# Two sums of value products moved by one step of ten on VectorE, in a decoder layer's output-projection group

## The chip, the cores and the metric

One core of one Trainium2 chip. The metric is the device time of one execution in microseconds (us); the time before the change is the median of three runs.

## The reference

A decoder layer over x of 8 batches x 512 tokens x 256 channels, in float32, three steps with a residual each:

```python
x = x + attn(layernorm(x), Wq, Wk, Wv, Wo)        # 16 heads, causal, complex-valued: q, k, v have 32 numbers a head
x = x + xattn(layernorm(x), ctx, ctx)             # per token: 16 query heads x 16 key heads, causal over heads
x = x + ffn(layernorm(x), kernel, bias, a, b)     # y = h @ int4(kernel) + bias + (h @ a) @ b
```

In `xattn` each token attends over its own 16 heads of 16 numbers: scores = q.k over the 16 numbers, masked so that head q sees keys k <= q, a softmax over k, and the sum of probability times value over k. No two tokens meet there.

## The kernel before, in words

One pass of `body(i, b)` runs per batch index i from -1 to 7, on every engine with the same structure (passes 3 to 5 are one hardware loop). A pass has four groups g of four attention heads each, and each group ten steps n, in which TensorE makes ten pairs of "units": one exponential unit (scores on the key side, for group g) and one maximum unit (scores on the query side, for the group after). Each batch is at several stages at once: in pass i, group 1 does the output projection of batch i-1's attention, the per-token attention (`xattn`) of the tiles of batches i-1 and i-2, and the projections of batch i+1.

The maxima. At step n >= 1 TensorE scores maximum unit n-1 into one of two PSUM banks (`scores`, L619), and VectorE takes its maximum in the same step (`take_max`, L1240, instruction L1251). TensorE scores unit u only after the maximum of unit u-2 has been taken (`max_taken`). Unit 9 is done in step 0 of the next group, and two small minima (L1312, L1313) finish the row. TensorE then turns the row (L659).

The split. At steps 1 and 2 TensorE projects q and k of the next heads into PSUM banks misc[0] and misc[1]; ScalarE copies the high part, and VectorE makes the low part at steps 2 and 3 (`low_part`, L1257: q_lo, k_lo). SyncE moves six pieces by DMA into stack_q and stack_k, where the maximum and exponential units read them. A bank of misc is taken by the next user only when its last reader is done (`take`, L528): in group 2 the value projection of step 3 (`project_v`, L605, writing misc<-w_hi,xt_hi) takes the bank that q_lo reads.

The per-token attention is shared between GpSimd and VectorE. GpSimd makes score products (L325), VectorE sums them (L1263, score_rows) at steps 5 and 8 and adds the mask to the diagonal blocks at step 9 (L1360, reads score_rows and head_mask), then takes the row maxima (L1382). GpSimd subtracts them (L1646), ScalarE does the exponential, VectorE sums and inverts (`tile_inverses`, L1279 and L1282, at step 2), GpSimd normalises (L1628) and makes the value products in four instructions, chunks 0 to 3 (L1633). VectorE sums these over the keys in the next group (`value_sums`, L1271, instruction L1263, head_out), chunk 3 first, and GpSimd adds head_out to x2 (`add_to_x2`, L1599, instruction L1601), which waits for the semaphore hpv_sum that VectorE raises after chunks 0 and 1. On GpSimd's queue that add stands ahead of the normalisation and the value products of the next tile.

The order of the work is written out by hand: each engine runs its own list in program order. In groups 0, 2 and 3 the value sums stand in step 0. In group 1 (`late_sums`, L1324) step 0 and step 1 also carry the adds of the output projection to x1 (L1288) and steps 1 and 2 the layernorm statistics of x1 (L1229, L1235, L1237), so there the value sums start at step 1. GpSimd turns the statistics into coefficients (`ln_coefficients`, L1562, ends with L1570) ahead of its add to x2. Passes 2 to 7 have value sums in group 1, six groups; pass 7 has no q and k projections, and so no q_lo and k_lo, in that group.

Of the kernel before, what the change touches and what calls it, by code (L numbers as in the profile page):

```python
# [97 lines left out]
def decoder_layer(nc, x, ctx_in, wq, wk, wv, wo, ffn_w, ffn_bias, ffn_a, ffn_b, out):  # L98
# [26 lines left out]
    def ok(b):  # L125
        return 0 <= b < N_BATCH

    with ExitStack() as ctx:
# [184 lines left out]
        def tiles(i, g):  # L313
            def tile(back):
                b, t = divmod(g - back, NT)
                return (b - 1, t) if ok(i + b - 1) else None
            return tile(2), tile(3), tile(4)
# [836 lines left out]
        def _(dve):  # L1154
# [68 lines left out]
            def ln_statistics(which, src, part):  # L1223

                if part == 0:

                    wait(dve, ln_scale[which], n_scale[which].up() - 1)
                for t in (2 * part, 2 * part + 1):
                    last = vec.bn_stats(ln_raw[:, which, t, :], src[:, t, :])  # L1229
                if part == 0:  # L1230
                    return
                last.then_inc(dve_own, 1)

                dve.wait_ge(dve_own, n_own.up())
                vec.tensor_copy(touched[:, which, :], ln_raw[:, which, 0, 0:1])  # L1235
                for t in range(NT):
                    last = vec.bn_aggr(ln_mv[:, which, t, :], ln_raw[:, which, t, :])  # L1237
                last.then_inc(ln_stats[which], 1)
# [32 lines left out]
            def value_sums(chunks):  # L1271
                return sum_products(
                    lambda j: head_out[:, j * 4 * HD:(j + 1) * 4 * HD],
                    lambda j: pv_prod[:, COFF[j]:COFF[j + 1]].rearrange("p (a k) -> p a k", k=4 * (j + 1)), chunks)
# [16 lines left out]
            def body(i, b):  # L1291
                for g in range(NG):
                    st = stages(i, g)
                    scored, attended, added = tiles(i, g)
                    for n in range(UNITS):
# [28 lines left out]
                        late_sums = g == 1 and ok(i - 1)  # L1324
# [11 lines left out]
                        if g == 1 and ok(i - 1) and n in (1, 2):  # L1336
                            dve.wait_ge(x1_added, n_wo.now(2 - n))
                            ln_statistics(1, x1, n - 1)
                        if added and n == (1 if late_sums else 0):
                            value_sums((2,))  # L1340
                        if added and n == (2 if late_sums else 0):
                            value_sums((0, 1)).then_inc(hpv_sum, 1)
                        if attended and n == 2:
                            tile_inverses()
# [154 lines left out]
            for c in range(CC):  # L1499
                last = vec.tensor_tensor(first_rows(by_row(w_lo, c)), first_rows(by_head(w_raw, c)),  # L1500
                                         f32(first_rows(by_row(w_hi, c))), ALU.subtract)
            last.then_inc(w_lo_ready, 1)
            turn.batches(dve, body, N_BATCH)


# [243 lines left out]
```

## Time and profile before

| | us |
|---|---|
| median of 3 runs | 806.22 |
| the runs | 806.05, 806.22, 807.44 |
| profiled execution | 807.63 |
| its span | 805.8 |
| TensorE busy | 746.7 |
| VectorE busy | 603.2 |
| GpSimd busy | 493.2 |
| ScalarE busy | 403.6 |

The profile is of one execution; its span runs from the first to the last instruction, and times on it are in us from the span's start. PE is TensorE, PEld its weight loads, DVE VectorE, ACT ScalarE, POOL GpSimd, SP SyncE. A row of a timeline gives the start, the time that the merged instructions cover, the engine, line, operation, output<-inputs, the count, and in brackets the idle time ahead of it with the one that ended it.

### The profile page before, as it was taken

To read this page: it belongs to the slowest core of one execution; us is meant where nothing else is said; L and a number is where in the kernel's file an instruction comes from. 1 tells how busy PE (TensorE), PEld (TensorE's weight loads), DVE (VectorE), ACT (ScalarE), POOL (GpSimd) and SP (SyncE) were. 2 spreads that over 40 slices of the span, in tenths; PEclk is the share of its full clock that TensorE was granted. 3 is DMA by queue.
4 is the path that set the end of the run, shared out by engine and by line. 5 is a ranking of instruction groups with operands and counts; after the bars stand their busy time and mean duration, and the time that the engine had idled before them with its cause. 6 is when DMAs were issued, how large, how long until landed. Compare 5 with 4: busy or idle time off the path is not lost.

```text
span 805.8 us, 16218 instructions
## 1 busy us (share of the span) xinstructions
PE 746.7 (93%) x5733; PEld 529.4 (66%) x5733; DVE 603.2 (75%) x1227; ACT 403.6 (50%) x760; POOL 493.2 (61%) x458
## 2 busy tenths in 40 slices
PE   8779899998999999999999999999999998889996
PEld 6656565765675656667666667576757674469996
DVE  3454555456686987698879987998698968699984
ACT  5114555554664557375736564756465545642111
POOL 5000000020876888598868887888878895986753
PEclk9979999999999999999999999999999998999999
DMA  5976666857784676577756775777567760100101
GB/s 186 127 94 106 81 80 86 138 77 90 92 131 70 93 96 86 99 98 116 96 98 89 114 96 95 99 115 98 82 87 113 100 98 8 60 8 14 34 14 39
DMA packets 47981, 70.55 MB, mean 88 GB/s; under 512 B 4897, under 2 KB 22578, under 8 KB 47922
## 3 DMA queue, kind: packets, MB, share of 16 engines
q1 hardware_dynamic: 46898, 69.52, 57.7%
q8 instruction: 35, 0.57, 0.3%
q10 hardware_dynamic: 1024, 0.26, 0.2%
q14 instruction: 24, 0.20, 0.1%
HBM read 14.98 MB, written 4.19 MB: 24 GB/s over the span
## 4 chain that ended last, share of the span: by engine, by line
PE 62%; DVE 15%; DMA 12%; issue 4%; ACT 3%; POOL 3%; SPq 1%; DVEq 0%; ACTq 0%; POOLq 0%
PE misc L542 22%; PE exp_bank L542 14%; DMA stack_k<-k_lo 10%; PE max_bank L542 10%; PE acc_bank L542 8%; PE sum_bank L542 7%; DVE head_out L1263 3%; DVE neg_max L1251 2%; DVE ln_raw L1229 2%; DMA stack_q<-max_row 1%; ACT x_in L932 1%; POOL prod L325 1%; DVE prod L370 1%; PE misc L592 1%; ACT probs L972 1%
## 5 line engine op out<-in xcount | busy, mean ns | idle before, releaser
L972 ACT ACTIVATE probs<-exp_bank 128x512 f32<-128x512 f32 x320 | 188.4, 594 | 172.5 <-PE exp_bank L542 101.5
L1251 DVE TENSOR_REDUCE neg_max<-max_bank 128x1 f32<-128x512 f32 (+1 forms) x192 | 129.2, 681 | 110.9 <-PE max_bank L542 110.3
L1633 POOL TENSOR_TENSOR prod<-head_probs,ctx_sb 128x256 f32<-128x256 f32 (+1 forms) x100 | 181.7, 1850 | 2.2 <-POOL head_probs L1628 0.5
L542 PE MATMUL max_bank<-stack_k,stack_q 96*128 96x384 f32 (+3 forms) x512 | 155.6, 366 | 24.0 <-DVE neg_max L1251 12.8
L542 PE MATMUL exp_bank<-stack_q,stack_k 97*128 97x384 f32 (+3 forms) x512 | 148.6, 352 | 14.5 <-ACT probs L972 10.8
L325 POOL TENSOR_TENSOR prod<-x1n,ctx_sb 128x256 f32<-128x256 f32 (+1 forms) x104 | 158.5, 1555 | 3.7 <-ACT x1n L932 3.7
L542 PE MATMUL acc_bank<-probs,values 128*32 128x512 f32 (+3 forms) x1024 | 152.7, 457 | 0.0
L542 PE MATMUL sum_bank<-probs,ones 128*32 128x512 f32 (+3 forms) x1024 | 150.5, 455 | 0.0
L1567 POOL TENSOR_TENSOR ln_var<-ln_mv,eps 128x4 f32<-128x4 f32 x21 | 4.4, 212 | 195.9 <-DVE ln_mv L1237 195.9
L1251 DVE TENSOR_REDUCE seg_max<-max_bank 128x4 f32<-128x512 f32 x128 | 86.6, 685 | 36.9 <-PE max_bank L542 35.6
L542 PEld LDWEIGHTS exp_bank<-stack_q,stack_k 97*128 97x128 f32 x512 | 84.0, 193 | 43.7 <-ACT probs L972 31.8
L542 PEld LDWEIGHTS max_bank<-stack_k,stack_q 96*128 96x128 f32 x512 | 86.6, 199 | 30.1 <-DVE neg_max L1251 14.7
L1263 DVE TENSOR_REDUCE score_rows<-prod 128x64 f32<-128x1024 f32 (+1 forms) x104 | 79.8, 808 | 8.9 <-POOL prod L325 8.9
L542 PE MATMUL max_bank<-mask_q,ident_b 128*128 128x256 bf16 (+1 forms) x320 | 84.8, 265 | 0.0
L542 PE MATMUL exp_bank<-mask_k,ident_b 128*128 128x256 bf16 (+1 forms) x320 | 84.3, 264 | 0.0
L1263 DVE TENSOR_REDUCE head_out<-prod 128x64 f32<-128x256 f32 (+2 forms) x100 | 75.6, 808 | 1.8 <-POOL prod L1633 1.8
L542 PEld LDWEIGHTS sum_bank<-probs,ones 128*32 128x32 f32 x1024 | 49.0, 112 | 39.2 <-issue 34.6
L542 PE MATMUL exp_bank<-prod,ident 128*128 128x160 f32 (+4 forms) x416 | 61.1, 307 | 3.6 <-POOL prod L370 2.6
L542 PEld LDWEIGHTS exp_bank<-prod,ident 128*128 128x128 f32 x416 | 58.8, 190 | 5.6 <-POOL prod L370 2.8
L542 PEld LDWEIGHTS acc_bank<-probs,values 128*32 128x32 f32 x1024 | 45.7, 112 | 23.4 <-issue 13.8
L542 PE MATMUL misc<-xt_hi,w_hi 128*128 128x512 f32 x128 | 56.8, 444 | 2.0 <-DVE xt_lo L1364 1.3
L1646 POOL TENSOR_TENSOR head_probs<-score_rows,head_max 128x256 f32<-128x256 f32 x26 | 16.3, 627 | 68.9 <-DVE head_max L1382 68.8
(186 smaller groups left out, 1392.6 us busy)
## 6 DMA issues: line engine op xcount, KB each, us to landing
stack_q<-q_hi SPq DMA_DIRECT2D x62, 256.0 KB, 5.6
stack_k<-k_hi SPq DMA_DIRECT2D x62, 256.0 KB, 9.3
stack_q<-q_lo SPq DMA_DIRECT2D x31, 256.0 KB, 6.9
stack_k<-k_lo SPq DMA_DIRECT2D x31, 256.0 KB, 10.5
x_in<-in_x SPq DMA_DIRECT2D x9, 512.0 KB, 5.6
ctx_sb<-in_ctx SPq DMA_DIRECT2D x32, 128.0 KB, 2.8
x<-in_x SPq DMA_DIRECT2D x7, 512.0 KB, 10.2
out<-y_sb SPq DMA_DIRECT2D x5, 512.0 KB, 3.2
```

Of the source, the lines that this page charges most:

```text
L325: last = engine.tensor_tensor(qk_prod[:, COFF[j]:COFF[j + 1]].rearrange("p (q k d) -> p q k d", q=4, d=HD), x1n[:, t, 4 * j * HD:4 * (j + ...
L370: last = engine.tensor_tensor(end_prod_qk[:, d0:d1, COFF[j] // HD:COFF[j + 1] // HD].rearrange("p d (q k) -> p d q k", q=4), end_x1n_turne ...
L542: return nc.tensor.matmul(*args, **kw)
L592: last = nc.tensor.transpose(bank[:, t * P:(t + 1) * P], src[:, t, c * P:(c + 1) * P], ident[:, :])
L932: last = nc.scalar.activation(dst[:, t, :], src[:, t, :], ACT.Identity, bias=ln_bias[:, which, t:t + 1], scale=ln_rstd[:, which, t:t + 1])
L972: nc.scalar.activation(probs[:, (UNITS * g + n) % PTR, :], exp_bank[n % 2][:, :], ACT.Exp, scale=SCALE).then_inc(exp_done, 1)
L1229: last = vec.bn_stats(ln_raw[:, which, t, :], src[:, t, :])
L1251: vec.tensor_reduce(o, v, axis=AX_X, op=ALU.max, negate=True).then_inc(max_taken, 1)
L1263: last = vec.tensor_reduce(out(j), products(j), axis=AX_X, op=ALU.add)
L1567: own(gp.tensor_tensor(ln_var[:, which, :], ln_mv[:, which, :, 1], eps[:, :], ALU.add))
L1633: last = gp.tensor_tensor(pv_prod[:, COFF[j]:COFF[j + 1]].rearrange("p (q d k) -> p q d k", q=4, k=keys), head_probs[:, 4 * j:4 * j + 4, N ...
L1646: gp.tensor_tensor(head_probs[:, :, :], head_scores[:, :, :], head_max[:, :, None].to_broadcast([P, NH, NH]), ALU.subtract).then_inc(h_shi ...
```

## The change

In group 1 the sum of chunk 2 moves from step 1 to step 2, and the sums of chunks 0 and 1 (with the semaphore hpv_sum) from step 2 to step 3. Chunk 3 stays in step 1 and the other groups stay as they are. The instructions are the same.

```diff
                         if g == 1 and ok(i - 1) and n in (1, 2):
                             dve.wait_ge(x1_added, n_wo.now(2 - n))
                             ln_statistics(1, x1, n - 1)
-                        if added and n == (1 if late_sums else 0):
+                        if added and n == (2 if late_sums else 0):
                             value_sums((2,))
-                        if added and n == (2 if late_sums else 0):
+                        if added and n == (3 if late_sums else 0):
                             value_sums((0, 1)).then_inc(hpv_sum, 1)
                         if attended and n == 2:
                             tile_inverses()
```

VectorE's instructions in group 1 of pass 2, from the end of the first statistics on, before the change. head_out<-prod is a value sum, neg_max<-max_bank the maximum of a unit (here 1, then 2), and a name in brackets is a semaphore:

```order
L1263 TENSOR_REDUCE head_out<-prod 128x64
L1251 TENSOR_REDUCE neg_max<-max_bank 128x1 [waits max_scored]
L1257 TENSOR_TENSOR q_lo<-misc,q_hi 128x512 [waits qk_hi_ready]
L1229 BN_STATS ln_raw<-x 128x6 [waits x1_added]
L1229 BN_STATS ln_raw<-x 128x6
L1235 COPY touched<-ln_raw 128x1 [waits dve_own]
L1237 BN_AGGR ln_mv<-ln_raw 128x2 x4
L1263 TENSOR_REDUCE head_out<-prod 128x64 x2
L1279 TENSOR_REDUCE head_sum<-head_probs 128x16 [waits h_exp]
L1282 RECIPROCAL head_inv<-head_sum 128x16 [waits hpv_prod,dve_own]
L1251 TENSOR_REDUCE neg_max<-max_bank 128x1 [waits max_scored]
L1257 TENSOR_TENSOR k_lo<-misc,k_hi 128x512 [waits qk_hi_ready]
```

The same place with the change:

```order
L1251 TENSOR_REDUCE neg_max<-max_bank 128x1 [waits max_scored]
L1257 TENSOR_TENSOR q_lo<-misc,q_hi 128x512 [waits qk_hi_ready]
L1229 BN_STATS ln_raw<-x 128x6 [waits x1_added]
L1229 BN_STATS ln_raw<-x 128x6
L1235 COPY touched<-ln_raw 128x1 [waits dve_own]
L1237 BN_AGGR ln_mv<-ln_raw 128x2 x4
L1263 TENSOR_REDUCE head_out<-prod 128x64
L1279 TENSOR_REDUCE head_sum<-head_probs 128x16 [waits h_exp]
L1282 RECIPROCAL head_inv<-head_sum 128x16 [waits hpv_prod,dve_own]
L1251 TENSOR_REDUCE neg_max<-max_bank 128x1 [waits max_scored]
L1257 TENSOR_TENSOR k_lo<-misc,k_hi 128x512 [waits qk_hi_ready]
L1263 TENSOR_REDUCE head_out<-prod 128x64 x2
```

Chunk 2 has moved from ahead of unit 1's maximum to behind the statistics, and chunks 0 and 1 from there to behind k_lo. Unit 3's maximum follows in both. Passes 3 to 6 have the same order.

VectorE in group 1 of pass 7, before the change, from the same point to unit 4's maximum (seg_max):

```order
L1263 TENSOR_REDUCE head_out<-prod 128x64
L1251 TENSOR_REDUCE neg_max<-max_bank 128x1 [waits max_scored]
L1229 BN_STATS ln_raw<-x 128x6 [waits x1_added]
L1229 BN_STATS ln_raw<-x 128x6
L1235 COPY touched<-ln_raw 128x1 [waits dve_own]
L1237 BN_AGGR ln_mv<-ln_raw 128x2 x4
L1263 TENSOR_REDUCE head_out<-prod 128x64 x2
L1279 TENSOR_REDUCE head_sum<-head_probs 128x16 [waits h_exp]
L1282 RECIPROCAL head_inv<-head_sum 128x16 [waits hpv_prod,dve_own]
L1251 TENSOR_REDUCE neg_max<-max_bank 128x1 [waits max_scored] x2
L1251 TENSOR_REDUCE seg_max<-max_bank 128x4 [waits max_scored]
```

And with the change:

```order
L1251 TENSOR_REDUCE neg_max<-max_bank 128x1 [waits max_scored]
L1229 BN_STATS ln_raw<-x 128x6 [waits x1_added]
L1229 BN_STATS ln_raw<-x 128x6
L1235 COPY touched<-ln_raw 128x1 [waits dve_own]
L1237 BN_AGGR ln_mv<-ln_raw 128x2 x4
L1263 TENSOR_REDUCE head_out<-prod 128x64
L1279 TENSOR_REDUCE head_sum<-head_probs 128x16 [waits h_exp]
L1282 RECIPROCAL head_inv<-head_sum 128x16 [waits hpv_prod,dve_own]
L1251 TENSOR_REDUCE neg_max<-max_bank 128x1 [waits max_scored]
L1263 TENSOR_REDUCE head_out<-prod 128x64 x2
L1251 TENSOR_REDUCE neg_max<-max_bank 128x1 [waits max_scored]
```

Without q_lo and k_lo the chunks 0 and 1 now stand between the maxima of units 2 and 3.

GpSimd in group 1 of pass 2, the same before and after: what stands behind its wait for hpv_sum.

```order
L1570 TENSOR_TENSOR ln_bias<-ln_negm,ln_rstd 128x4 [waits pool_own]
L1601 TENSOR_TENSOR x<-x,head_out 128x256 [waits hpv_sum]
L1628 TENSOR_TENSOR head_probs<-head_probs,head_inv 128x256 [waits h_inv]
L1633 TENSOR_TENSOR prod<-head_probs,ctx_sb 128x256 [waits hpv_sum,pool_own]
L1633 TENSOR_TENSOR prod<-head_probs,ctx_sb 128x512
L1633 TENSOR_TENSOR prod<-head_probs,ctx_sb 128x768
L1633 TENSOR_TENSOR prod<-head_probs,ctx_sb 128x1024
L1646 TENSOR_TENSOR head_probs<-score_rows,head_max 128x256 [waits h_max,hpv_prod]
```

Nothing moved on this queue; the semaphore that L1601 waits for is raised at another place of VectorE's list.

## Rows read from the trace of the kernel before

**Rows 1.** The page, busy time of each engine.

```profile
PE 746.7 (93%) x5733; PEld 529.4 (66%) x5733; DVE 603.2 (75%) x1227; ACT 403.6 (50%) x760; POOL 493.2 (61%) x458
```

**Rows 2.** Waits: engine, tile, line <- what ended it: total us, times, longest.

```profile
PE max_bank L542 <- DVE neg_max L1251: 12.8, 10, 2.2
```

**Rows 3.** Timeline of TensorE, pass 3, groups 1 and 2.

```profile
336.00 0.23 PE L542 MATMUL max_bank<-mask_q,ident_b 128*128 128x128 bf16 x1
...
340.85 0.51 PE L542 MATMUL max_bank<-stack_k,stack_q 96*128 96x384 f32 x2 [1.37 <-DVE neg_max L1251]
...
343.27 0.50 PE L542 MATMUL exp_bank<-stack_q,stack_k 97*128 97x384 f32 x2
...
345.54 0.48 PE L542 MATMUL max_bank<-stack_k,stack_q 96*128 96x384 f32 x2
...
350.72 0.49 PE L542 MATMUL max_bank<-stack_k,stack_q 96*128 96x512 f32 x1 [0.32 <-DMA stack_k<-k_lo]
...
356.48 0.36 PE L542 MATMUL misc<-w_hi,xt_hi 128*128 128x256 f32 x1
```

**Rows 4.** Timeline of VectorE, pass 3, groups 1 and 2.

```profile
335.48 0.94 DVE L1263 TENSOR_REDUCE head_out<-prod 128x64 f32<-128x768 f32 x1
336.33 0.68 DVE L1251 TENSOR_REDUCE neg_max<-max_bank 128x1 f32<-128x512 f32 x1
...
338.66 0.98 DVE L1263 TENSOR_REDUCE head_out<-prod 128x64 f32<-128x256 f32 x2
...
340.71 0.68 DVE L1257 TENSOR_TENSOR k_lo<-misc,k_hi 128x512 fp32r<-128x512 f32 x1
341.31 0.68 DVE L1251 TENSOR_REDUCE neg_max<-max_bank 128x1 f32<-128x512 f32 x1
...
344.49 0.68 DVE L1251 TENSOR_REDUCE seg_max<-max_bank 128x4 f32<-128x512 f32 x1
...
348.99 0.36 DVE L1360 TENSOR_TENSOR score_rows<-score_rows,head_mask 128x64 f32<-128x64 f32 x1
349.27 0.68 DVE L1368 TENSOR_TENSOR x2t_lo<-misc,x2t_hi 128x512 fp32r<-128x512 f32 x1
...
355.21 0.68 DVE L1257 TENSOR_TENSOR q_lo<-misc,q_hi 128x512 fp32r<-128x512 f32 x1
```

**Rows 5.** Stretches of group 1: us, busy time of each engine, PEclk, DMA share, GB/s.

```profile
257.50:259.50 2.00, 2.00 (x12) 0.40 (x8) 2.00 (x4) 1.20 (x3) 1.98 (x2) 0.50 1.08 127
342.00:344.00 2.00, 2.00 (x22) 0.78 (x12) 2.00 (x3) 1.99 (x5) 2.00 (x2) 1.00 1.06 123
425.00:427.00 2.00, 2.00 (x16) 0.42 (x8) 2.00 (x3) 1.24 (x3) 2.00 (x3) 0.50 1.06 126
...
674.00:676.00 2.00, 2.00 (x16) 0.37 (x8) 1.90 (x2) 0.82 (x2) 2.00 (x2) 0.50 0.00 0
```

**Rows 6.** Timeline of TensorE, pass 4, group 1.

```profile
423.62 0.50 PE L542 MATMUL max_bank<-stack_k,stack_q 96*128 96x384 f32 x2 [1.38 <-DVE neg_max L1251]
...
427.73 0.50 PE L542 MATMUL exp_bank<-stack_q,stack_k 97*128 97x384 f32 x2
```

**Rows 7.** Timeline of GpSimd, pass 3, group 1.

```profile
340.59 0.73 POOL L1601 TENSOR_TENSOR x<-x,head_out 128x256 f32<-128x256 f32 x1
...
346.35 2.91 POOL L1633 TENSOR_TENSOR prod<-head_probs,ctx_sb 128x1024 f32<-128x1024 f32 x1
```

**Rows 8.** Line L1360: engine, op, tile, count: min/median/max ns, first and last start.

```profile
L1360 DVE TENSOR_TENSOR score_rows<-score_rows,head_mask x26: 213/216/1768, 201.5 to 711.1; 128x64 f32<-128x64 f32 x26
```

**Rows 9.** Timelines of TensorE and VectorE, pass 7, group 1.

```profile
666.53 0.23 PE L542 MATMUL max_bank<-mask_q,ident_b 128*128 128x128 bf16 x1
...
672.16 0.80 PE L542 MATMUL max_bank<-stack_k,stack_q 96*128 96x384 f32 x2 [2.20 <-DVE neg_max L1251]
...
668.23 0.68 DVE L1251 TENSOR_REDUCE neg_max<-max_bank 128x1 f32<-128x512 f32 x1
...
671.47 1.22 DVE L1251 TENSOR_REDUCE neg_max<-max_bank 128x1 f32<-128x512 f32 x2
```

## The prediction

> **What bounds the kernel.** TensorE is busy 93% of the span and VectorE 75% [rows 1], so a microsecond is won or lost where TensorE stands still. I read the list of waits first: among those for VectorE that hold TensorE back, the longest group is scores for the maxima that wait for an earlier maximum, 12.8 us in 10 waits [rows 2]. The timeline of TensorE then places them: one wait of 1.37 us in the output-projection group (group 1), here of pass 3, before unit 4's scores at 340.85 [rows 3]. Six passes, 2 to 7, run this group with value sums in it. Unit 4 writes the bank that unit 2's maximum has to leave first. The timeline of VectorE shows that maximum behind everything else [rows 4]: its neighbour k_lo starts at 340.71, and VectorE stands idle nowhere between unit 0's maximum and the end of the group.
>
> One more thing differs between the passes, the granted clock of TensorE behind that wait. In passes 2, 4 and 7 it is 0.50 (1.2 GHz), in pass 3 it is 1.00 (2.4 GHz), and passes 5 and 6 read like 3 [rows 5]. From unit 4's scores to the next exponential scores pass 3 needs 343.27 - 340.85 = 2.42 us [rows 3] and pass 4 427.73 - 423.62 = 4.11 us [rows 6]. The slow passes have 1.7 us more of TensorE's time, and VectorE catches up in it. So they are costed apart.
>
> **The first move: chunk 2 behind unit 1's maximum.** The sum of chunk 2 starts at 335.48 and unit 1's maximum at 336.33, so it holds VectorE for 0.85 us [rows 4]. Taking it from in front of that maximum looks like a gain of 0.85. But the last matmul of unit 1 starts at 336.00 and lasts 0.23 us [rows 3]: the maximum cannot start before about 336.27. It gains 0.06 us, and the rest becomes a hole in VectorE. What follows is as long as before, since chunk 2 (0.85) now stands where chunks 0 and 1 (0.98 as listed, about 0.90 to the next start) stood (an instruction's listed time overlaps the next start by some 0.09, as 335.48 + 0.94 - 336.33). Unit 2's maximum comes 0.06 + 0.05 = 0.11 us earlier. The wait of 1.37 us shrinks to 1.26. Pass 4 gains that much too, pass 2 nearly nothing: together 0.15 us. In the other full-speed passes it is lost again, below.
>
> **The second move: chunks 0 and 1 behind k_lo.** k_lo stays where it is (0.1 us earlier), then come 0.90 us of sums, so unit 3's maximum and all that follows on VectorE is 0.79 us late. Two things hang on it.
>
> (a) GpSimd. Its add of head_out to x2 waits for hpv_sum, and the normalisation and the four value products stand behind it on the same queue. The add started at 340.59 [rows 7]. The sums now end at 340.60 + 0.60 + 0.90 = 342.10 (k_lo to the next start, 341.31 - 340.71 [rows 4], then the sums); with 0.2 for the handover, my estimate, the add starts at 342.3: 1.7 us later. GpSimd's idle time in this group lies ahead of the layernorm coefficients, which do not move, and covers none of it. The last product, 346.35 for 2.91 us, ended at 349.26 [rows 7] and now ends at 350.97.
>
> (b) The mask add, L1360, on VectorE. In 26 executions it takes 0.216 us in the median and up to 1.77 [rows 8]. In pass 3 it began at 348.99 and took 0.36, to 349.35, and the next instruction began at 349.27, at the very end of GpSimd's last product, 349.26 [rows 4, 7]. So it waits for a GpSimd product in progress. After the change it is due at 349.78 with that product running until 350.97: it blocks, and the next instruction begins at 350.98 in place of 349.27, 1.71 us late. The Trainium skill ("SBUF — State Buffer", section "Who interferes with whom") has this as a rule: a VectorE instruction with two SBUF inputs contends with a GpSimd instruction that reads SBUF, and whichever issued second blocks for the whole instruction. By that rule and the ends of rows 4 and 7, the trace agrees; without it the sum would be near zero (rival 1).
>
> **What this costs TensorE.** From there VectorE has no idle time until q_lo of group 2, at 355.21 for 0.68 [rows 4], which moves with the lag of 1.65 to 1.71 us and ends at about 357.55. The value projection of group 2 takes the PSUM bank that q_lo reads; it started at 356.48 [rows 3]. It now waits until 357.59: TensorE is 1.1 us late, whatever smaller waits came before. Behind it unit 3's scores set VectorE's pace again, so the loss does not grow. It is paid three times, in passes 3, 5 and 6: 3.3 us, less in pass 6 (I take 0.9), so 3.1 us.
>
> In passes 2 and 4 the half clock gives VectorE its 0.79 us back before unit 5. GpSimd is still late by 1.7 us and L1360 waits some tenths, but its successor, unit 9's maximum, waits for TensorE there. Cost 0, gain 0.15. If that cover went they would cost 1.1 each.
>
> Pass 7 has no projections between the units. Unit 1's scores were complete at 666.53 + 0.23, and its maximum started only at 668.23 [rows 9]. There the move works: chunk 2's 0.85 us disappears from in front of it, unit 2's maximum (671.47) moves by 0.9, and with it unit 4's scores (672.16, after a wait of 2.20). k_lo does not exist in this pass, so GpSimd is only 0.4 late. The chain runs over this wait into the tail, so I count 0.9 us of gain.
>
> **The sum:** + 3.1 - 0.15 - 0.9 = + 2.05 us. The profiled execution took 807.63 us (span 805.8), 1.4 more than the median of the runs, 806.22. With the same pattern of clocks it would take 809.7; set against the median it gives 808.3 us. The unknown price is the block of L1360: from 0 (it slips in between two products; TensorE then loses only what the 0.79 does, below) to the 1.2 us from 349.78 to 350.97, and the matching rows give nearly all of it. Below zero is excluded, since no work was removed.
>
> **Rivals.**
> 1. No block, or a block that is covered; time unchanged. Then only the 0.79 us counts. Unit 5's maximum (344.49, 0.68 long) ends at 345.97 in place of 345.17, and unit 7's scores, at 345.54 in pass 3 [rows 3, 4], and the transposes behind them slip by about 0.6; but TensorE waited 0.32 us for the stack's DMA at 350.72 [rows 3], so 0.3 us is left, three times: + 0.9 - 1.05 = about 806.1 us. For: the margins are tenths. Against: L1360's end in three passes. 0.30.
> 2. Faster: the hole is not there. If unit 1's scores are ready for the maximum in every pass, as in pass 7, unit 2's maximum moves by 0.9 in all six and pulls unit 4: 5.4 us less, 800.8 us. It decides at the point where TensorE finishes unit 1 before VectorE finishes the statistics. Against: rows 3 put it 0.06 us before, in all of passes 2 to 6. Between this and the forecast lies a pass that stays at full clock for once; 1.7 us each. 0.15 in all.
> 3. Slower than forecast: the granted clock falls in more groups. New short waits of TensorE (at unit 7, the maxima's turn and the value projection) stand behind one of 1.3 us. The Trainium skill ("TensorE: Matmul & The Clock Gate", section "What's actually happening") says "the default state is throttled, and activity releases the throttle". By that rule less busy stretches may be granted less; in rows 5 and 6 equal waits were followed by either level. A pass that turns pays 1.7 in place of 1.1, and all three give + 1.8: 810.1 us. 0.10.
>
> The forecast itself has 0.45.
>
> **Numbers.** 808.3 us is the likeliest. The range has to reach to rival 1 with its own scatter (one pass more or less at half clock is 1.7 us), so from 804.8, and to rival 3, 810.4; the forecast's own part is 807.0 to 809.8. A measurement of this kernel can tell about 0.2% (1.6 us) from no change. Slower by more than that: most of the forecast (0.40) and rival 3 (0.10), 0.50. Within: rival 1 (0.28) and the low edge of the forecast (0.05), 0.33. Faster: rival 2 (0.15) and the edge of rival 1 (0.02), 0.17.
>
> **What would show it.** Right, step by step: in the full-clock passes a hole of about 0.7 us on VectorE ahead of unit 1's maximum; unit 4's wait 0.1 shorter; GpSimd's add 1.7 us later; L1360 longer than 1 us in group 1; a wait for q_lo ahead of group 2's value projection; unit 4's wait in pass 7 down to about 1.3. It is wrong if L1360 stays at 0.2 to 0.4 us there, if the projection starts without a wait, or if the passes at half clock are others and many.

## The result: slower by 0.65%, with the profile after

The median went from 807.44 us (five runs beside the changed kernel, 806.05 to 807.83) to 811.32 us (five runs, 809.74 to 814.15): ratio 1.0065, 95% interval 1.0043 to 1.0087. I had forecast 808.3 us, 2.1 above the median that I had, with 810.4 as the upper end. The sign was right, and the time lies above the range. It is 3.0 us above the forecast in two parts: the kernel before is itself 1.2 us above the median of three runs that I built on (807.44 against 806.22), and the change costs 3.9 us in place of 2.1. Beside the twelve kernels of the experiments the kernel before ran 87 times more; one execution took 2428.69 us and is left out below, and the other 86 have a median of 806.96 us.

The waits of the profiled execution (809.74 us, span 807.9), in the columns of [rows 2]:

```profile
PE max_bank L542 <- DVE neg_max L1251: 10.9, 9, 1.8
...
PE misc L659 <- DVE neg_max L1313: 2.3, 5, 0.7
...
POOL x L1601 <- DVE head_out L1263: 9.8, 6, 1.8
```

The group of [rows 2] fell from 12.8 to 10.9 us. The waits for unit 9's minima went from one of 0.5 us to five with 2.3 us in all. New are GpSimd's six waits for the value sums, 1.8 us at most.

VectorE in pass 3, the timeline that answers to [rows 4]:

```profile
331.80 0.69 DVE L1251 TENSOR_REDUCE neg_max<-max_bank 128x1 f32<-128x512 f32 x1 [0.70 <-PE max_bank L542]
...
334.14 0.92 DVE L1263 TENSOR_REDUCE head_out<-prod 128x64 f32<-128x768 f32 x1
...
336.14 0.68 DVE L1257 TENSOR_TENSOR k_lo<-misc,k_hi 128x512 fp32r<-128x512 f32 x1
336.73 1.00 DVE L1263 TENSOR_REDUCE head_out<-prod 128x64 f32<-128x256 f32 x2
...
345.33 1.25 DVE L1360 TENSOR_TENSOR score_rows<-score_rows,head_mask 128x64 f32<-128x64 f32 x1
346.51 0.68 DVE L1368 TENSOR_TENSOR x2t_lo<-misc,x2t_hi 128x512 fp32r<-128x512 f32 x1
...
352.40 0.68 DVE L1257 TENSOR_TENSOR q_lo<-misc,q_hi 128x512 fp32r<-128x512 f32 x1
```

There is the hole of 0.70 us ahead of unit 1's maximum, and the mask add of 1.25 us in place of 0.36. GpSimd beside it, which answers to [rows 7]:

```profile
337.82 0.73 POOL L1601 TENSOR_TENSOR x<-x,head_out 128x256 f32<-128x256 f32 x1 [1.69 <-DVE head_out L1263]
338.51 0.62 POOL L1628 TENSOR_TENSOR head_probs<-head_probs,head_inv 128x256 f32<-128x256 f32 x1
339.20 7.30 POOL L1633 TENSOR_TENSOR prod<-head_probs,ctx_sb 128x256 f32<-128x256 f32 x4
```

The four products end at 339.20 + 7.30 = 346.50, and the instruction behind the mask add starts at 346.51. TensorE, against [rows 3]:

```profile
336.28 0.50 PE L542 MATMUL max_bank<-stack_k,stack_q 96*128 96x384 f32 x2 [1.26 <-DVE neg_max L1251]
341.57 0.51 PE L542 MATMUL max_bank<-stack_k,stack_q 96*128 96x384 f32 x2 [0.36 <-DVE seg_max L1251]
348.44 0.28 PE L659 MATMUL misc<-ident,neg_max 128*16 128x128 f32 x1 [0.41 <-DVE neg_max L1313]
353.13 0.38 PE L542 MATMUL misc<-w_hi,xt_hi 128*128 128x256 f32 x1 [0.21 <-DVE q_lo L1257]
```

Unit 4's wait is 0.11 shorter, as worked out, and three waits behind it take more than that. To compare passes I use one **stretch**: from the start of the turned row (L659) in group 1 to the first value projection in group 2. Each row below is that stretch in one of the passes 2 to 6 (columns as in [rows 5]). The kernel before:

```profile
249.50:272.96 23.46, 21.79 (x150) 12.94 (x151) 20.98 (x43) 14.18 (x28) 16.71 (x16) 0.93 0.58 83
333.83:356.48 22.65, 20.96 (x158) 13.65 (x159) 22.55 (x47) 14.98 (x30) 16.24 (x15) 1.00 0.61 87
416.60:440.42 23.82, 22.44 (x158) 13.79 (x159) 22.22 (x45) 15.08 (x30) 15.93 (x15) 0.93 0.57 81
500.54:523.10 22.56, 20.95 (x158) 13.65 (x159) 22.46 (x46) 15.00 (x30) 16.15 (x15) 1.00 0.60 85
583.39:606.11 22.72, 20.97 (x158) 13.64 (x159) 22.46 (x46) 15.01 (x30) 16.37 (x15) 1.00 0.61 87
```

And the changed kernel:

```profile
247.47:270.69 23.22, 20.66 (x151) 12.90 (x151) 22.27 (x43) 14.57 (x29) 15.58 (x15) 1.00 0.61 87
329.36:353.13 23.77, 21.53 (x158) 13.82 (x158) 22.96 (x45) 15.51 (x31) 15.72 (x15) 1.00 0.60 84
414.90:438.63 23.73, 21.50 (x158) 13.81 (x158) 22.93 (x45) 15.51 (x31) 15.68 (x15) 1.00 0.59 83
500.40:524.16 23.76, 21.52 (x158) 13.81 (x158) 22.96 (x45) 15.51 (x31) 15.71 (x15) 1.00 0.59 83
586.08:609.82 23.74, 21.47 (x158) 13.72 (x158) 22.83 (x45) 15.63 (x31) 15.61 (x15) 1.00 0.60 85
```

In pass 3 the stretch grew by 23.77 - 22.65 = 1.12 us, where I had worked out 1.1; passes 5 and 6 grew by 1.20 and 1.02. The surprise is the clock: before, passes 2 and 4 held half-clock time (mean 0.93), and now none of the five does. Passes 2 and 4 take 0.24 and 0.09 us less than before, although they are back at full clock: what the clock gave back, the changed order took. Against the old order at full clock (22.65 in pass 3) all five stretches are longer. In pass 7 the gain came: unit 4's scores stand behind a wait of 1.40 in place of 2.20 [rows 9]. The way to them is counted from VectorE's second add to x1:

```profile
665.00 0.68 DVE L1288 TENSOR_TENSOR x<-x,misc 128x512 f32<-128x512 f32 x1
```

That is before the change. The changed kernel has it, and unit 4's scores, at:

```profile
668.61 0.68 DVE L1288 TENSOR_TENSOR x<-x,misc 128x512 f32<-128x512 f32 x1
...
674.86 0.50 PE L542 MATMUL max_bank<-stack_k,stack_q 96*128 96x384 f32 x2 [1.40 <-DVE neg_max L1251]
```

The half clock did not vanish. In pass 7 it still stands in group 1, and it appears in group 3 of passes 3 to 5, about a microsecond after waits of 0.7 and 0.5 us for ScalarE that the kernel before has too, at full clock. The changed kernel in pass 3:

```profile
382.50:386.00 3.50, 3.50 (x34) 1.46 (x33) 2.48 (x10) 0.60 (x1) 1.26 (x4) 0.51 0.45 77
```

### The profile page after: what moved, and what is told of

It reads as the page before. It is cut to its first block, busy times and chain, and to the rows that moved or that the text cites. A ratio compares the mean times of both kernels' runs of the same rounds, so it can differ in the third digit from the quotient of the medians.

```text
span 807.9 us, 16218 instructions
## 1 busy us (share of the span) xinstructions
PE 747.7 (93%) x5733; PEld 530.3 (66%) x5733; DVE 606.2 (75%) x1227; ACT 403.8 (50%) x760; POOL 493.5 (61%) x458
## 4 chain that ended last, share of the span: by engine, by line
PE 58%; DVE 21%; DMA 8%; issue 5%; POOL 3%; ACT 3%; SPq 1%; DVEq 0%; ACTq 0%; POOLq 0%
PE misc L542 21%; PE exp_bank L542 14%; PE max_bank L542 9%; PE acc_bank L542 7%; DMA stack_k<-k_lo 7%; PE sum_bank L542 6%; DVE neg_max L1251 3%; DVE head_out L1263 3%; DVE seg_max L1251 2%; DVE score_rows L1263 2%; DVE ln_raw L1229 1%; ACT x_in L932 1%; POOL prod L325 1%; DMA stack_q<-max_row 1%; DVE prod L370 1%
## 5 line engine op out<-in xcount | busy, mean ns | idle before, releaser
L542 PE MATMUL max_bank<-stack_k,stack_q 96*128 96x384 f32 (+3 forms) x512 | 155.9, 366 | 23.0 <-DVE neg_max L1251 10.9
L542 PEld LDWEIGHTS exp_bank<-mask_k,ident_b 128*128 128x128 bf16 x320 | 31.0, 97 | 35.9 <-issue 26.8
```

The lines of the kernel that those rows point to most:

```text
L542: return nc.tensor.matmul(*args, **kw)
```

## Experiments

The ratio of each kernel is to the runs of the kernel before beside it, 28 or 29 of them.

**1 to 4. One move at a time, and the mask add taken out.** Kernel e1 makes the first move alone, e2 the second alone:

```diff
-                        if added and n == (1 if late_sums else 0):
+                        if added and n == (2 if late_sums else 0):
                             value_sums((2,))
```

```diff
-                        if added and n == (2 if late_sums else 0):
+                        if added and n == (3 if late_sums else 0):
                             value_sums((0, 1)).then_inc(hpv_sum, 1)
```

e3 is the change and e4 the kernel before, each with this edit, which leaves out the masking of group 1's tiles. The maximum that stands in for the add reads one input:

```diff
-                            vec.tensor_tensor(own_heads, own_heads, head_mask[:, None, 0:4, 0:4]
-                                              .to_broadcast([P, CHUNKS, 4, 4]), ALU.add).then_inc(h_masked, 1)
+                            if g == 1:
+                                vec.tensor_reduce(spare[:, :], head_scores[:, 0:4, 0:4], axis=AX_X,
+                                                  op=ALU.max).then_inc(h_masked, 1)
+                            else:
...
```

> The first move alone: chunk 2 in step 2, chunks 0 and 1 stay there too. Both theories agree on VectorE: a hole of 0.7 us ahead of unit 1's maximum, everything behind it 0.79 us late, unit 4's wait on TensorE up from 1.37 to about 2.15 us. The theory of the lags (each microsecond that VectorE is late at q_lo of group 2 comes back on TensorE) gives 0.5 us a pass at full clock and 0.8 at half clock: 809.9 to 811.5 us. The theory that the granted clock alone made the time (the lags only shift when TensorE's short waits come) gives either sign, within 2 us of before.

> The second move alone: chunks 0 and 1 in step 3, chunk 2 stays in step 1 in front of unit 1's maximum, where VectorE would otherwise wait. Unit 2's maximum should come 0.9 us earlier and unit 4's wait fall from 1.37 to 0.5 us; GpSimd's add 0.9 late; the mask add L1360 blocks until about 0.9 us later than before. The theory of the lags gives + 0.3 us a pass at full clock, - 0.9 at half clock, - 0.9 in pass 7: 805.5 to 807.5 us, no loss. The rival that GpSimd's lateness by itself is what costs gives a loss of half of the change's, some 2 us: 809.5. The clock theory gives anything between.

> The change with the mask add L1360 of group 1 left out (a reduce of 4 columns with one input stands in its place, so the tiles of that group are not masked). If the block of L1360 by GpSimd's product is a term of the loss, the second low part of x2 starts about 1.2 us earlier, the wait ahead of group 2's value projection is gone and each pass at full clock is 0.8 us shorter: 807.5 to 809 us against 811.3 of the change. If the 0.79 us of lateness alone makes the loss, the time stays within 0.5 us of the change's.

> The kernel before with the same mask add left out, as the control for the one above. Before, the add was held by 0.15 us in the passes at full clock and nothing waited for it: within 0.7 us of before, 806.7 to 808.1, by either theory. If it gains 2 us or more, the mask add itself bound the kernel and not its meeting with the product.

| kernel | median us, runs | ratio, 95% interval |
|---|---|---|
| e1, first move | 815.99, 6 | 1.0108, 1.0072 to 1.0145 |
| e2, second move | 806.38, 12 | 0.9989, 0.9969 to 1.0010 |
| e3, change, no mask add | 807.38, 12 | 0.9993, 0.9974 to 1.0012 |
| e4, before, no mask add | 807.12, 12 | 0.9994, 0.9971 to 1.0017 |

e3 against e4: without the two-input add in group 1 the loss is gone, and the control did not move. e3 came out 0.1 below its range, far from the 811.3 of the rival, and e4 is in its range. VectorE in pass 4 of e3, and the stretch around it:

```profile
430.83 0.16 DVE L1362 TENSOR_REDUCE spare<-score_rows 128x4 f32<-128x16 f32 x1
```

```profile
414.88:437.69 22.81, 21.19 (x158) 13.70 (x159) 22.02 (x45) 15.10 (x30) 15.72 (x15) 1.00 0.60 85
```

GpSimd's four products run there until 424.69 + 7.27 = 431.96, so the maximum with one input took 0.16 us in the middle of a product that blocks the add. The hole and the 0.79 us of lateness are still in e3: at full clock they cost about 0.2 us a pass (22.81 against 22.6).

e2 is in its range, and the rival that GpSimd's lateness by itself costs some 2 us is out. It also says that the block alone does not decide either. Its mask add is blocked as long as in the change, and yet the projection starts without a wait. TensorE in pass 3 of e2:

```profile
331.03 0.28 PE L659 MATMUL misc<-ident,neg_max 128*16 128x128 f32 x1 [0.36 <-DVE x L1288]
...
337.13 0.50 PE L542 MATMUL max_bank<-stack_k,stack_q 96*128 96x384 f32 x2 [0.46 <-DVE neg_max L1251]
...
353.95 0.39 PE L542 MATMUL misc<-w_hi,xt_hi 128*128 128x256 f32 x1
```

VectorE in the same pass of e2:

```profile
346.19 1.21 DVE L1360 TENSOR_TENSOR score_rows<-score_rows,head_mask 128x64 f32<-128x64 f32 x1
```

Here chunks 0 and 1 left the place ahead of unit 2's maximum with nothing put there, so unit 4's wait fell by 0.9 (1.37 to 0.46) and unit 3's maximum was not late. The stretch is 353.95 - 331.03 = 22.92, 0.27 longer than before. Before, q_lo was done 0.6 us ahead of the projection (355.89 against 356.48, [rows 3, 4]). Lateness of 0.79 alone (e3) or a block that adds 0.9 alone (e2) nearly fits into that (0.2 and 0.3 us a pass); the change has both, 1.65 to 1.7, and pays 1.1.

e1 missed by 4.5 us, and the other theory, within 2 us of before, missed by more. Its mask add is not blocked (0.21 us), unit 4's wait grew to 2.18, and all five stretches held half-clock time. Those of passes 2 and 3 of e1:

```profile
248.57:273.87 25.30, 23.12 (x150) 13.99 (x151) 21.05 (x43) 14.18 (x28) 16.53 (x15) 0.87 0.54 77
333.04:357.60 24.56, 22.38 (x158) 13.78 (x159) 22.32 (x45) 15.09 (x30) 15.87 (x15) 0.93 0.56 80
```

The five stretches of e1 sum to 123.55 us and those of the kernel before to 115.21, which is the whole difference of 8.3 us between the two profiled spans (814.1 and 805.8).

The mean granted clock of e1's runs is 0.965 in place of 0.975. From it I work out a **clock loss** for any run, span x (1 - clock). The lower level is 0.50, so the time spent at it is twice the clock loss, and the clock loss is the most that it can have added to the span: where TensorE would have waited anyway, it adds less. The clock loss of e1 is 28.3 us on average against 20.1 before. So up to 8.2 of the 9.7 us between the mean spans (814.97 and 805.28) are the clock.

**5 to 7 and a control. Moving the mask add, and more of the dose.** e5 (the change), e6 (the second move) and e9 (before) have the mask add and the head maxima of group 1 behind unit 9's maximum and minima:

```diff
+                        if g == 2 and n == 0 and tiles(i, 1)[0]:
+                            dve.wait_ge(hqk_sum, n_masked.up())
...
-                        if scored and n == 9:
+                        if scored and g != 1 and n == 9:
```

e7 is the change with chunks 0 and 1 one step later still: `n == (4 if late_sums else 0)`.

> The change, with group 1's mask add and head maxima moved from step 9 to step 0 of group 2, behind unit 9's maximum and the two minima. Nothing is left out. Theory (the blocked mask add is the term): by pass 3 of the profile of the change GpSimd's last value product ends at 346.50 and unit 9's maximum and the minima would end about 347.2, so the add takes 0.21 to 0.25 us everywhere in group 1 of passes 2 to 6, the wait ahead of the value projection shrinks below 0.1, and 1.0 x 5 goes: 806 to 808 us, like the kernel before. GpSimd's subtraction starts within 0.3 us of where it does now (347.59). Rival (what e3 took away was the mask add's own work and place, or the 0.79 us of lateness is what costs): 809.5 us or more.

> The second move alone (chunk 2 stays in step 1, chunks 0 and 1 in step 3), with group 1's mask add and head maxima moved behind unit 9's maximum and the minima. Nothing is left out. In the second move alone the add was blocked for about 1.0 us too (1.21 at 346.19) and TensorE hardly waited for q_lo behind it (0.2 us, once). Theory: that block was nearly covered there, so 804.8 to 806.6 us, at most 1.5 below the second move alone. Rival (the block costs wherever it stands, and the second move alone gained elsewhere what it lost there): 5 x 0.8 to 1.0 less, 801.5 to 803 us.

> The kernel before, with group 1's mask add and head maxima moved behind unit 9's maximum and the minima: the control of the two kernels with that move. Nothing is left out. Theory: the add took 0.2 to 0.4 us in group 1 before, so only the few tenths at its end and the 0.2 us of GpSimd's handover count: 805.5 to 807.5 us, no change that can be told. Rival (the new place is better or worse by itself, whatever GpSimd does): outside 804.5 to 808.5 us, and then the two other kernels say nothing on the block.

> The change, with the sums of chunks 0 and 1 (and their semaphore) another step later, in step 4 behind unit 3's maximum. Theory: GpSimd's add is another 0.6 to 0.7 us later, its last value product ends at about 347.15 in pass 3, the mask add takes about 1.9 us in place of 1.25, TensorE loses another 0.6 us in each of five passes or so: 813.5 to 816 us. Rival (what costs is VectorE's lateness at units 3 to 5, not the block): unit 3's maximum is 0.9 us earlier here, so 806.5 to 810 us.

| kernel | median us, runs | ratio, 95% interval |
|---|---|---|
| e5, change, mask later | 808.76, 12 | 1.0027, 1.0010 to 1.0044 |
| e6, second move, mask later | 807.58, 12 | 1.0010, 0.9993 to 1.0027 |
| e9, before, mask later | 809.12, 12 | 1.0030, 1.0007 to 1.0052 |
| e7, one step more | 815.98, 6 | 1.0104, 1.0072 to 1.0136 |

e7 hit, in time and in place: the add of head_out waits 2.28 us, the mask add takes 1.82, and the stretch is 359.87 - 335.55 = 24.32 us, 0.55 above the change for 0.57 more of block. GpSimd and VectorE in pass 3 of e7:

```profile
344.58 0.74 POOL L1601 TENSOR_TENSOR x<-x,head_out 128x256 f32<-128x256 f32 x1 [2.28 <-DVE head_out L1263]
```

```profile
351.51 1.82 DVE L1360 TENSOR_TENSOR score_rows<-score_rows,head_mask 128x64 f32<-128x64 f32 x1
```

e5 missed by 0.8 us, and its control e9 missed by 1.6 and is as slow, so by the terms set beforehand the two medians say nothing on the block. What their profiles show is where each stands. In e5 the add is free of GpSimd (0.22), but with it gone VectorE stands idle for TensorE, and the add and the maxima now stand behind that hole, in front of q_lo. VectorE in pass 3 of e5:

```profile
347.06 0.69 DVE L1251 TENSOR_REDUCE neg_max<-max_bank 128x2 f32<-128x512 f32 x1 [0.35 <-PE max_bank L542]
...
347.93 0.22 DVE L1317 TENSOR_TENSOR score_rows<-score_rows,head_mask 128x64 f32<-128x64 f32 x1
```

Its stretch is 23.31 us (330.05 to 353.36), with a wait of 0.28 for q_lo. So taking the block away here is worth 0.46, not all of the 1.1. e9's full-clock stretches are 22.62 to 22.65 us, no longer than before. Its two half-clock ones are (24.26 and 24.21 against 23.82), again with 0.28 for q_lo, and its runs have more clock loss (23.0 us against 19.9 in the runs beside it); what puts it there is open. e6 missed its range by 1.0, upwards: its stretches of 22.59 to 22.65 us are 0.2 to 0.3 shorter than e2's in passes 3 to 6, as the theory wants, but its runs have 22.0 us of clock loss against e2's 18.4, enough to eat the gain.

**8 and 10 to 12. The terms one by one.** e10 makes both moves in pass 7 alone, e11 in passes 2 to 6 alone (`2 if i == 7 else 1` and `3 if i == 7 else 2`, or the reverse, in the two conditions). e8 is e7 with the edit of e3. e12 puts parts together: e6's edits in passes 2 to 6, both moves in pass 7.

> Both moves in pass 7 alone; passes 2 to 6 as before. Theory (the terms of the sum stand apart): passes 2 to 6 read like before, 22.6 to 22.7 us from the turned row of group 1 to the value projection of group 2 where the clock is full, unit 4's wait in pass 7 is 1.3 to 1.4 us in place of 2.2, and the 0.9 us of gain reaches the end: 805.3 to 806.8 us beside a before of 806.8 to 807.1. Rival (the tail gives the gain back, since other engines set its end): 806.8 to 808 us, with the end as far behind pass 7's group 1 as before plus 0.9.

> Both moves in passes 2 to 6; pass 7 as before. Theory (every one of the five passes pays 1.1 us where its group 1 runs at full clock, as all five do in the profile of the change): the same distance is 23.7 to 23.8 us in passes 3 to 6, mask add over 1.2 us, and the time is 5.5 above before: 811.3 to 813.5 us, about 0.9 above the change itself. Rival (three passes pay, as I forecast, and the rest of the 4 us is the clock of other groups): 809 to 810.8 us.

> Chunks 0 and 1 in step 4, as in the kernel with one step more, and group 1's mask add replaced by a maximum with one input (group 1's tiles are left unmasked): the control of that kernel. Theory: without an instruction that meets GpSimd's product the place of the sums costs nothing, 22.6 to 23.0 us from the turned row to the value projection, 806.3 to 808.5 us, 7 to 9 less than with the mask add. Rival (the place of the sums costs by itself, by GpSimd's later products or by unit 3's neighbours): 810 us or more.

> A version of parts: in passes 2 to 6 the second move alone with the mask add and head maxima behind unit 9's maximum and the minima, in pass 7 both moves with the mask add in its place. Nothing is left out. Theory: 22.60 to 22.65 us from the turned row to the value projection in passes 2 to 6, as in the kernel with that edit (0.05 to 0.1 less than before), and 0.9 less in pass 7: 804.5 to 806.8 us, if the clock falls no more often than before. Rival (what the clock takes differs by the order, as in the runs of the second move with the mask later, 0.973 in place of 0.975): 806.8 to 808.3 us.

| kernel | median us, runs | ratio, 95% interval |
|---|---|---|
| e10, pass 7 alone | 805.85, 12 | 0.9999, 0.9979 to 1.0019 |
| e11, passes 2 to 6 | 812.16, 6 | 1.0075, 1.0048 to 1.0103 |
| e8, one step more, no mask add | 805.31, 12 | 0.9984, 0.9967 to 1.0001 |
| e12, parts together | 805.57, 12 | 1.0005, 0.9983 to 1.0027 |

e8 against e7 is the clearest pair: the same order, 10.7 us apart (they ran beside different runs of the kernel before: ratios 1.0104 and 0.9984), with the stretch of pass 3 at 22.84 us in place of 24.32:

```profile
330.99:353.83 22.84, 21.20 (x159) 13.68 (x159) 22.03 (x45) 15.12 (x30) 15.14 (x15) 1.00 0.60 86
```

```profile
346.96 0.16 DVE L1362 TENSOR_REDUCE spare<-score_rows 128x4 f32<-128x16 f32 x1
```

In passes 2 to 5, at full clock in both, the stretches are 1.17, 1.48, 1.50 and 1.49 us shorter, 5.6 in all; pass 6 of e8 held half-clock time. The clock loss of the runs differs by 3.8 (18.8 and 22.5). e8 came out 1.0 below its range. The place of the sums costs next to nothing; the instruction that meets GpSimd's product turns it into time.

e11 holds the test of the step on which the forecast failed. Its median is in the range of the theory that five passes pay, above the 810.8 us of the rival with three; the lower end of its ratio's interval, 1.0048, still allows 810.3. Its pass 4 fell to half clock in group 1, and its pass 5 did not; the stretches of the two:

```profile
413.78:437.54 23.76, 22.49 (x159) 13.88 (x159) 22.53 (x45) 15.32 (x31) 15.71 (x15) 0.93 0.57 81
497.68:521.41 23.73, 21.55 (x158) 13.81 (x158) 22.93 (x45) 15.49 (x31) 15.70 (x15) 1.00 0.59 83
```

And the mask add in that pass 4:

```profile
430.36 0.63 DVE L1360 TENSOR_TENSOR score_rows<-score_rows,head_mask 128x64 f32<-128x64 f32 x1
```

At half clock the changed order takes 23.76 us and the order before 23.82, with the add blocked by 0.4. That half-clock pass pays nothing, as I had put it; it is one stretch in one profile. Read the other way, half clock adds 0.03 us to this stretch in the changed order (23.76 against 23.73) and 1.2 in the order before (23.82 against 22.6). Taking it as certain which passes those are was the mistake.

e10's profile has unit 4's wait in pass 7 at 1.41, but its ratio cannot be told from 1. e10 and e12 are both in their ranges, and neither is shown to beat the kernel before: the gains that their profiles promise (0.9 us, and at most 0.1 a pass) are smaller than what the clock moves from run to run.

## Why the prediction was wrong in size

- **The first move** was right: hole of 0.70, unit 4's wait 0.11 shorter.
- **The second move (a)** was right: GpSimd stood 1.69 us ahead of the add of head_out. **(b)** was right: the mask add blocked to 346.50, 1.25 us long. The Trainium skill's rule ("SBUF — State Buffer", section "Who interferes with whom") held in e3 and e8 as well: with one SBUF input in place of two the instruction took 0.16 us with GpSimd's product in progress.
- **1.1 us a pass** was right at full clock: 1.12 in pass 3, 23.76 - 22.56 = 1.20 in pass 5, 23.74 - 22.72 = 1.02 in pass 6. That a pass costs 0 at half clock was right for pass 4 (e11); no profile has pass 2 of the changed order at half clock.
- **Pass 7's 0.9** was right: from the second add to x1 to unit 4's scores it was 7.16 us (672.16 - 665.00) and is 6.25 (674.86 - 668.61). It reaches the end: from that add to the end of the span the change takes 139.3 us and e11, which leaves pass 7 alone, 140.3.
- **The step that failed** is the count of passes, "It is paid three times, in passes 3, 5 and 6", with "Cost 0, gain 0.15" for passes 2 and 4. It took the half clock of one execution for a property of those passes. In the profile of the change none of the passes 2 to 6 had half-clock time in group 1. Against the order before at full clock, pass 4 pays 23.73 - 22.6 = 1.1 as well (22.6 is an estimate from passes 3 and 5; no profile has that order in pass 4 at full clock), and pass 2, where the order before takes 22.65 (e9), pays 0.6. The sum by these stretches is 1.12 + 1.1 + 1.20 + 1.02 + 0.57 - 0.9 = + 4.1 us. The two medians of five runs differ by 3.9, and the interval of the ratio is 3.5 to 7.0 us.
- That this sum fits is in part argued: of the other four runs only the mean clock is on record, not where it fell. What is shown is one profile of the change and one of e11, in which nine of ten stretches are at full clock and long.
- I had this as "If that cover went they would cost 1.1 each", and gave it no case of its own. Rival 3 named the clock, but with the opposite sign: passes turning to half clock. Rivals 2 and 3 also priced such a turn at 1.7 us, which is neither the 1.2 of the order before nor the 0.03 of the changed one.
- **The base** was a second error, of 1.2 us: a median of three runs. With the five runs beside the changed kernel the same sum gives 809.5 us, and on the old base the measured 3.9 us would have been 810.1, inside the range.

The profiled pair by itself would have misled. Its spans differ by 807.9 - 805.8 = 2.1 us, just my 2.05, and nearly term by term: 1.12 + 1.20 + 1.02 in passes 3, 5 and 6, less 0.24 and 0.09 in passes 2 and 4, less 0.9 in pass 7. But that was the fastest of the five executions of the change, with a clock of 0.979 against 0.975 before, a clock loss of 17.0 us against 20.1. Over the runs the two kernels have nearly the same, 19.6 and 20.1 us. So the change did not buy clock. In its profile the half clock stands outside the stretches where it had covered VectorE's lateness.

## What to carry to other kernels

When an instruction is moved later, follow the queue behind the semaphore that it raises, up to the point where the delayed work meets an instruction of the first engine that contends with it: here 0.9 us of sums came back as 0.9 us of blocked mask add. Each of the two latenesses alone nearly fitted into the 0.6 us of slack ahead of the value projection (0.2 and 0.3 us a pass), and both together did not (1.1). A cover that hangs on the granted clock may be gone in the changed kernel: cost every pass at either level, and give the case without the cover a price and a chance. Take the clock as a sum over many runs. Where a few drops of the clock more or less move a run by several us, compare a stretch at equal clock, pass by pass, ahead of medians.

## What the runs showed of the hardware

How often group 1 (passes 2 to 6) held half-clock time goes with TensorE's wait ahead of unit 4. In the fourteen profiles, by that wait in pass 3: 2.18 us, 5 of 5 stretches (e1); 1.37 to 1.38, 7 of 20 (before, e4, e9, e10); 1.26 to 1.27, 5 of 30 (the change, e3, e5, e7, e8, e11); 0.46, 0 of 15 (e2, e6, e12). Equal waits were followed by either level of the clock, 1.2 or 2.4 GHz. In the four profiles with the old order in passes 2 to 6 (before, e4, e9, e10) pass 4 held half-clock time each time, passes 3 and 5 never and passes 2 and 6 now and then; with unit 4's wait at 1.26 us it was pass 4 twice and passes 3, 5 and 6 once each. So the places are not quite random for one order, and they move when the order changes. The Trainium skill ("TensorE: Matmul & The Clock Gate", section "What's actually happening") says that the gate's window is free-running, so that the same kernel differs from run to run. The runs agree: the mean clock of the kernel before went from 0.966 to 0.981 in its 86 runs. In the counts above a longer wait is more often followed by the lower level, but only the ends, 0 of 15 and 5 of 5, stand clear of each other; 1.26 and 1.37 us cannot be told apart, and the stretches of one profile hang together.

Fewer such drops in group 1 did not mean fewer overall: e2, e6 and e12 had none there in their profiles, and their runs have 18.4, 22.0 and 21.2 us of clock loss. Only e1, where every group 1 had one, stands clearly apart. Why the drops of the changed kernel stand in group 3, behind waits that were there before, stays open.
